# A fused two-layer transformer kernel on one Trainium2 core: a norm's first half in pieces among attention steps, pieces at wider spacing, and totals inverted by way of VectorE transposes

## What is computed

```
x = x + _L0_attn_a_ref(_layernorm(x, axis=-1), ...)      # 16 heads, one shared key and value head
x = x + _L0_ffn_ref(_layernorm(x, axis=-1), weight, bias)
x = x + _L0_attn_b_ref(_layernorm(x, axis=-1), ...)      # 16 heads, causal
x = x + _L0_ffn_ref(_layernorm(x, axis=-1), weight, bias)
x = x + _L1_attn_a_ref(_layernorm(x, axis=-1), ...)      # latent attention, causal
...
def _L0_ffn_ref(x, weight, bias):
    xq, xs = _mx_quantize(x2)    # each block of 32 numbers: scale by its largest, round to a 6-bit grid
    out = (xq * xs) @ (wq * ws).T + bias
```

## Time and profile before

| | |
|---|---|
| median of 3 runs | 2655.19 us (2645.19 to 2660.45) |
| the profiled execution | 2647.86 us; its span, first to last instruction, 2646.1 us |
| busy, share of the span | PE 93%, DVE 64%, POOL 47%, ACT 46% |
| mean granted clock of PE | 0.961 of full |

### The profile page before, as it was taken

The page is one execution under the profiler, slowest core; times in us unless marked ns, Lnnn a source line. Parts: engine busy times, 40 slices in busy tenths (PEclk is TensorE's granted clock), DMA queues, the critical chain, the costliest instruction groups (busy, mean ns, idle before and its releaser), DMA issues. The chain is left out here.

```text
span 2646.1 us, 48410 instructions
## 1 busy us (share of the span) xinstructions
PE 2468.2 (93%) x19961; PEld 1286.4 (49%) x19961; DVE 1681.6 (64%) x2159; ACT 1210.4 (46%) x1815; POOL 1241.5 (47%) x812
## 2 busy tenths in 40 slices
PE   4899999989999999999995699999989999999989
PEld 2344444434444444555552466666554555555545
DVE  2577767886765765666667366766444666666654
ACT  2454445545444535444442244444424455555541
POOL 2577777767776444555552000000004555555540
PEclk8899999999999999999996599999999999999989
DMA  4000000000000000000000100000000000000000
GB/s 109 1 1 1 1 1 1 1 1 1 1 1 3 9 1 1 1 1 1 1 1 0 32 3 2 3 2 3 1 1 1 1 1 1 1 1 1 1 1 17
DMA packets 19184, 14.07 MB, mean 5 GB/s; under 512 B 3090, under 2 KB 17811, under 8 KB 18836
## 3 DMA queue, kind: packets, MB, share of 16 engines
q1 hardware_dynamic: 18964, 10.97, 1.7%
HBM read 9.39 MB, written 1.57 MB: 4 GB/s over the span
## 5 line engine op out<-in xcount | busy, mean ns | idle before, releaser
L1370 POOL TENSOR_TENSOR sums<-sums,p 128x1024 f32<-128x1024 f32 (+3 forms) x384 | 816.7, 2127 | 371.2 <-PE ps L1026 330.6
L1208 DVE TENSOR_REDUCE half_max<-ps 128x2 f32<-128x1024 f32 (+3 forms) x384 | 442.0, 1151 | 333.3 <-PE ps L1007 320.6
L1110 ACT ACTIVATE p<-ps 128x1024 f32<-128x1024 f32 (+3 forms) x384 | 347.5, 917 | 220.7 <-PE ps L986 161.8
L983 PE MATMUL ps<-q,k 64*128 64x512 f32 (+3 forms) x1792 | 428.1, 556 | 0.0
L776 POOL TENSOR_TENSOR sums<-sums,p 128x1024 f32<-128x1024 f32 (+3 forms) x160 | 277.7, 1735 | 188.1 <-PE ps L544 170.9
L1026 PE MATMUL ps<-p,v 128*64 128x512 f32 (+3 forms) x1536 | 340.3, 558 | 0.0
L986 PE MATMUL ps<-max_row,pick 64*128 64x512 f32 (+3 forms) x896 | 327.2, 727 | 0.0
L1229 DVE RECIPROCAL inverse<-total 128x128 f32<-128x128 f32 x256 | 240.5, 942 | 15.6 <-ACT total L1148 12.0
L1007 PE MATMUL ps<-k_near,q_near 64*128 64x512 f32 (+2 forms) x896 | 200.2, 443 | 35.0 <-DVE half_max L1208 34.6
L1592 ACT ACTIVATE p<-ps 128x2048 f32<-128x2048 f32 (+1 forms) x80 | 136.6, 1708 | 161.8 <-PE ps L1495 90.8
L692 DVE TENSOR_REDUCE half_max<-ps 128x2 f32<-128x1024 f32 (+3 forms) x128 | 129.2, 1009 | 121.3 <-PE ps L525 106.9
(11 more groups left out here) (269 smaller groups left out, 3955.2 us busy)
## 6 DMA issues: line engine op xcount, KB each, us to landing
q_w<-in_wq SPq DMA_DIRECT2D x3, 512.0 KB
o_w<-in_wo SPq DMA_DIRECT2D x3, 512.0 KB
k_w<-in_wk SPq DMA_DIRECT2D x2, 512.0 KB
v_w<-in_wv SPq DMA_DIRECT2D x2, 512.0 KB
out<-x SPq DMA_DIRECT2D x4, 256.0 KB, 2.3
scratch<-in_wq_t SPq DMA_DIRECT2D x1, 512.0 KB, 5.3
scratch<-in_w_out SPq DMA_DIRECT2D x1, 512.0 KB, 7.5
gate<-in_gate SPq DMA_DIRECT2D x1, 320.0 KB
```

The source lines that it names most:

```text
L983: nc.tensor.matmul(out[:, head, 0:width], a.k[rows, owner(i) % 3, k * P:(k + 1) * P], a.q[rows, i % 3, s * BANK + lo:(s + 1) * BANK], star ...
L1110: act.activation(probabilities(g)[:, :, lo:BANK], score[g % 2][:, :, 0:BANK - lo], ACT.Exp)\
L1208: last = v.tensor_reduce(out, chunk_ps[:, :, 0:hi - lo], AX.X, ALU.max, negate=True)
L1370: pool.tensor_tensor(sums, sums, probabilities(g)[:, :, lo:BANK], ALU.add).then_inc(summed, 1)
```

## The change

**First part.** The list `norms` now also has the last item of a1 with b = 0. The linear layer and norm of sequence 0 behind a1 (the first half of what n2 did) are strewn over steps of a1's items 24 to 31, beginning at step 10 of item 24. `norm_phase("n2")` gets `first=GROUPS // B` and does groups 2 and 3 alone: one pair in place of two.

**Second part.** The fixed tables become functions. `quantise_at` places a piece every second step for the first and the third norm and two pieces in three steps for the second (`HALVES`); what follows the pieces moves back as much: the first norm's "turn" 0 from step 36 to step 61, the second's to step 48. All stays at the same distances from one another behind the last piece.

**Third part.** `invert` no longer divides 128 x 512 numbers. DVE transposes `a.total` in blocks of 32 x 32 (`turn_total`), takes the reciprocal of one column of each block (128 x 16, `invert`), and transposes these back with each column repeated 32 times (`spread_inverse`), in the first two of the four steps. `normalise` stays where it was. ACT's next copy into `a.total` waits for the first transpose only. a3 is changed in the same way; the latent attention isn't.

```diff
+        HALVES = (4, 3, 4)
+        def quantise_at(n, piece):
+            return 9 + piece * HALVES[n] // 2
+        def norm_uses(n):
+            at = quantise_at(n, 25)
+            return {("turn", 0): at + 2, ("turn", 1): at + 4, ("line", 0): at + 6, ("line", 1): at + 8,
+                    ("turn", 2): at + 17, ("turn", 3): at + 19}
...
-            if n + 1 < len(layers) and pair == PAIRS - 1:
+            if (n + 1 < len(layers) or b + 1 < B) and pair == PAIRS - 1:
                 norms.append((begins[i] + when(i)["out", 1], b, i))
...
-                        act.wait_ge(inverted, QUARTERS * unit(i, part))
+                        act.wait_ge(total_turned, unit(i, part))
                     last = act.activation(a.total[:], small, ACT.Copy)
...
-            def invert(i, s, quarter):
...
-                v.reciprocal(a.inverse[:, cols], a.total[:, cols]).then_inc(inverted, 1)
+            def turn_total(i, s):
...
+                v.transpose(a.turned[:], a.total[:]).then_inc(total_turned, 1)
+            def invert(i, s):
...
+                v.reciprocal(a.inverses[:], a.turned[:].rearrange("p (b q) -> p b q", q=QB)[:, :, 0])\
+                    .then_inc(inverted, 1)
+            def spread_inverse(i, s):
...
+                v.transpose(a.inverse[:].rearrange("p (b q) -> p b q", q=QB),
+                            a.inverses[:].unsqueeze(2).to_broadcast([P, BANK // QB, QB])).then_inc(spread, 1)
...
-                    for quarter in range(QUARTERS):
-                        inverts_at[at + quarter] = (i, s, quarter)
-                    norms_at[at + QUARTERS] = (i, s)
+                    turns_at[at] = (i, s)
+                    inverts_at[at + 1] = (i, s)
+                    norms_at[at + 4] = (i, s)
...
-        norm_phase(nc, m, "n2", linear=True)
+        norm_phase(nc, m, "n2", linear=True, first=GROUPS // B)
```

More of the change, by code:

```diff
@@ L271, in normed_by @@
         def normed_by(n, g):
-            return GROUPS // 2 * n + g // 2 + 1
+            return (GROUPS - first) // 2 * n + (g - first) // 2 + 1
+        groups, some_tiles, used = range(first, GROUPS), range(first * TPG, TILES), slice(first * TPG, TILES)
         @block.tensor
@@ L282, in _ @@
             if linear:
-                for pair in range(0, GROUPS, 2):
+                for pair in groups[::2]:
                     for g in (pair, pair + 1):
-                        pe.wait_ge(quantised, g + 1)
+                        pe.wait_ge(quantised, g - first + 1)
                         turn(g)
                     for g in (pair, pair + 1):
-                        pe.wait_ge(copied, g + 1)
+                        pe.wait_ge(copied, g - first + 1)
                         nc.tensor.matmul(m.ps[:, g, :], m.ones_row[:], m.ffn_bias[:], start=True, stop=False)
@@ L294, in _ @@
                         last.then_inc(product, 1)
-            for g in range(GROUPS):
+            for g in groups:
                 pe.wait_ge(normed[g % 2], normed_by(int(linear), g))
@@ L303, in measure @@
             def measure(add, n):
-                for g in range(GROUPS):
+                for g in groups:
                     tiles = slice(g * TPG, (g + 1) * TPG)
                     if add:
-                        dve.wait_ge(product, g + 1)
+                        dve.wait_ge(product, g - first + 1)
                         link(nc.vector.tensor_tensor(m.x[:, tiles, :], m.x[:, tiles, :],
@@ L329, in _ @@
             if linear:
-                for g in range(0, GROUPS, 2):
+                for g in groups[::2]:
                     normalise(g + 1)
@@ L337, in _ @@
                 measure(True, 1)
-            for g in range(1, GROUPS, 2):
+            for g in groups[1::2]:
                 normalise(g)
@@ L344, in _ @@
                 act.wait_ge(var_ready, n + 1)
-                nc.scalar.activation(var[:], var[:], ACT.Sqrt).then_inc(std_ready, 1)
+                nc.scalar.activation(var[:, used], var[:, used], ACT.Sqrt).then_inc(std_ready, 1)
                 act.wait_ge(shift_ready, n + 1)
-                for g in range(0, GROUPS, 2):
+                for g in groups[::2]:
                     if n:
-                        act.wait_ge(turned, g + 1)
+                        act.wait_ge(turned, g - first + 1)
                     for t in range(g * TPG, (g + 1) * TPG):
@@ L353, in _ @@
                     last.then_inc(normed[0], 1)
-                for g in range(GROUPS):
-                    act.wait_ge(turned, n * GROUPS + g + 1)
+                for g in groups:
+                    act.wait_ge(turned, n * len(groups) + g - first + 1)
                     nc.scalar.activation(m.xn_t[:, g * BANK:(g + 1) * BANK], m.ps[:, 4 + g, :], ACT.Copy)\
@@ L926, in stream_phase @@
         for n, (start, _, _) in enumerate(norms):
-            for (kind, part), at in NORM_DVE.items():
+            for (kind, part), at in norm_dve(n).items():
                 dve_at.setdefault(start + at, []).append((kind, n, part))
-            for (kind, part), at in NORM_ACT.items():
+            for (kind, part), at in norm_act(n).items():
                 act_at.setdefault(start + at, []).append((kind, n, part))
```

98 lines of the change are left out of this document (64 added, 34 removed).

## The result

| | kernel before | changed kernel |
|---|---|---|
| median of 5 runs each, side by side | 2658.81 us (2645.19 to 2661.29) | 2639.03 us (2629.70 to 2639.77) |
| profiled execution, span | 2647.86, 2646.1 us | 2638.08, 2636.4 us |
| mean granted clock | 0.961 | 0.960 |

The ratio is 0.9931 (95% interval 0.9902 to 0.9959): 0.7% faster. The medians lie 19.8 us apart, the two profiled spans only 9.7. The kernel before has executions of two kinds, near 2645 us and near 2655 to 2661; its profiled one is of the quicker kind, the changed kernel's is at its median.

The account below looks back on a forecast made before the run. PE was taken to bound plain steps, DVE's chain n2. The terms -18.7 + 2 + 20 - 9.2 - 7.8 - 3.8 = -17.5 us took the median from 2655.2 to 2637.7 us; range 2616 to 2658.

Parts of the forecast that it names:

- clock term: Latent phase's start: four first projections slower at half clock, as n2 loses a burst of matmuls; +2 us, bounds 0 to +4.4.
- third norm: Items 24 to 31 of a1: the norm moved into the stream adds 20 us, bounds 12 and 30.3.
- n2: Phase behind the stream: removing half its work saves 18.7 us, leaving some 35.5 us.
- The sign that I had named: n2, from first statistics to the latent phase's first matmul: above 40 us would show the clock term wrong.
- rival 2: Norm tails: relief of DVE reaches them too, third norm costs 15 us; total 2627 us, 17% chance.
- rival 1: Stream: third norm costs 30.3 us through low clock, other relief at lower bounds; total 2650 to 2659 us, 27% chance.
- First norm: In a0: cost falls from 24.2 to 15 us (start 3, pieces 2, tail 10); saved 9.2, bounds 4 and 14.
- The sum for it: Item 10 of a0: DVE's 31.82 us plain work plus 16 pieces of up to 1.53 us makes 56.3 us.
- Second norm: In a1: tail keeps 17.5 of 19.5 us, the earlier 10.8 become 5; saved 7.8, bounds 2 and 14.
- Transposes: Inverting of the totals on DVE: 0.65 us each, running free of POOL if not two-port.
- Rival 3: Inverting steps: transposes slow or blocked by POOL, over 1.7 us each, making the kernel slower; 11% chance.
- Ends: Last steps of the stream and of a3: inverting falls from 3.39 to about 1.5 us; 3.8 us saved in all.

Follow-up runs that it names:

- e5_warm: Changed kernel plus 23 matmuls that nobody reads, placed where PE waits in n2 and before the latent attention's first scores: 2629.48 us, ratio to before 0.9908.
- e10_warmer: Changed kernel plus 42 matmuls that nobody reads, in n2 and behind every chunk and projection before the latent attention's first scores: 2624.38 us, ratio to before 0.9887.
- e1_no_third: Changed kernel without its first part (n2 with both pairs, no third norm in the stream): 2635.3 us, ratio to before 0.9914.
- e4_third_alone: Kernel before with only the first part of the change, a piece in every step and totals inverted in quarters: 2659.42 us, ratio to before 1.0019.
- e2_quarters: Changed kernel with the totals inverted in four quarters again instead of by transposes: 2642.04 us, ratio to before 0.9942.
- e3_tight: Changed kernel with a piece in every step again, transposes and third norm kept: 2649.19 us, ratio to before 0.9977.
- e7_no_root: Changed kernel with ACT's square root in the stream's norms replaced by a copy, so no table loads: 2629.54 us, ratio to before 0.9908.

## Why the prediction was right, and where its terms were off

2637.7 was forecast and 2639.03 measured, with faster as the likeliest. The parts did what they were said to do, but that the sum came out so near is in part luck. It was made on the profiled execution, 2646.1 - 17.5, and the two profiled spans lie only 9.7 us apart. The clock term was 7.9 us too small and the experts' 3.7 us were not in the sum; against them the third norm was 3.5 to 4.5 us cheaper than its term, and item 6 and the plain items gave 2.2. The medians lie 19.8 apart, 10 us more than the spans, and which part of that is the change's no trace shows. Point by point:

- **n2.** 35.5 us forecast, 1453.81 - 1418.22 = 35.6 in the trace. The term of 18.7 stands.
- **Clock behind n2.** Forecast +2, bounds 0 and +4.4; between the two profiled executions it was +9.9. This is the term that was mis-sized most. Its mechanism stands: with one pair the rise of the clock at n2's end is gone, in all eight traces without added matmuls. But I counted four projections at half clock, and the clock stayed at 0.50 through all the chunks and into the first scores, 61 us; e5_warm and e10_warmer show that this is what costs. The sign that I had named, n2 above 40 us, couldn't show it, since it looks at the phase's first matmul only. How much of the +9.9 the shortened n2 makes isn't settled: with one pair the phase took 402.5 to 407.3 us, with two 397.2 and 401.8, so it is between 0.7 and 10.1.
- **Third norm.** Forecast +20, bounds 12 and 30.3; 16.5 by the trace against e1_no_third. Items 29 to 31 (with the stream's end) are 1.33 + 10.81 + 2.64 = 14.8 above e1_no_third's, for 18, midway to rival 2's 12: the waits of its tail are shorter than the second's, probably as the projections of a next item are absent (not tried). With tight pieces and quarters it costs 25.9 (e4_third_alone), towards rival 1.
- **First norm.** Saved 7.8 for 9.2: start and pieces 5.5 us for 5, the tail 11.2 for 10. The prediction gave the saving to spacing and transposes together; e2_quarters and e3_tight show that it is the spacing's alone. The sum for it, 56.3 us of DVE's work in an item that took 55.5, was wrong and its agreement chance: it took all 16 pieces at the mean of the longest kind, and the trace of before has DVE busy for 45.93 us there (37.03 in the changed kernel, for 39.5). The wait behind the single piece, 2.83 us long, was the right reading.
- **Second norm.** Saved 8.2 for 7.8; the tail kept 17.7 for 17.5, with the same 2.29 us behind ACT's root; without the root it keeps 14.3 (e7_no_root). Here either half of the change would nearly have done: 22.4 us with transposes alone, 24.9 with spacing alone.
- **Transposes.** 0.701 and 0.712 us for 0.65, with POOL at work or not (all 128 lie between 0.698 and 0.712; `normalise` goes on at 1.688 us beside the 0.69 that it takes at the stream's end, with POOL idle). Rival 3 is out. By the Trainium skill (SBUF — State Buffer, "Who interferes with whom") a VectorE instruction with at most one SBUF input, outside the two-port modes, is free of GpSimd; the trace agrees.
- **Ends.** Forecast -3.8. Between before and the changed kernel a3 gave 2.5, and the stream's end, by e1_no_third's 37.4 us for 38.1, 0.8: 3.3. Against e2_quarters it is 2.4 and 2.0: 4.4.

Rival 1 (2650 to 2659) needed a third norm of 30; it had 16.5. Rival 2 (2627) needed relief in the tails; the second's kept its price, and the third norm, 16.5, came near to rival 2's 15.

## What to carry to other kernels

Work moved from a short phase bound by one engine into steps that another engine fills isn't hidden: here n2 gave back 15.6 to 18.5 us and the attention took 16.5 to 20.3, so nothing was won; it pays to price both sides, and to look at what lies between. When a queue has plain work and pieces, spread the pieces by the steps in which the plain work is light: tight spacing cost 10 us, and pieces that always meet another piece in the same step leave it no room to grow (16 us when that one doubled). After a stretch in which PE waits, look at the granted clock of what follows; 23 matmuls that nobody reads gave 8 to 10 us here (e5_warm), where the whole first part gave nothing.

## What was unexpected in the hardware

- The clock stayed at 0.50 for 106 us, though PE was busy 23.82 of 30 us in one part of it, at that clock. With 25.23 of 30 it was 0.95 in e10_warmer, so the profile's busy share hardly tells the two apart.
- A float32 transpose of 128 x 512 in blocks of 32 x 32 costs DVE 0.70 us, and 0.71 when its input is one column repeated 32 times. The reciprocal of 128 x 16 costs 0.247, of 128 x 128 0.942.
- A phase with the same instructions took 397.2 to 407.3 us in ten traces, and another 87.9 to 91.6, by how long the clock stood at 0.50 in it. In a comparison of two profiles that looks like a cost or a gain of the change; the clock of each phase shows it.
